# Two-layer FFN with split float32 weights: W2's high and low parts side by side in one matmul

## The reference

```python
t = cond(x)                                     # linear in x, per lane of 4 quaternion components
probs = softmax(t @ Wr.T)
h = gelu(t @ W1[7] + b1[7])                     # 256 -> 1024
out = x + (h @ W2[7] + b2[7]) * probs[:, 7:8]   # 1024 -> 256
```

## Time and profile before

| | us |
|---|---|
| median of three executions (lowest, highest) | 123.6 (123.53, 124.6) |
| span of the profiled execution, first to last instruction | 122.0 |
| TensorE matmul busy / weight loads busy | 104.4 / 92.1 |
| VectorE, ScalarE, GpSimd busy | 60.0, 49.7, 51.2 |

### The profile page before, as it was taken

The page is one execution under the profiler, slowest core; times in us unless marked ns, Lnnn a source line. Parts: engine busy times, 40 slices in busy tenths (PEclk is TensorE's granted clock), DMA queues, the critical chain, the costliest instruction groups (busy, mean ns, idle before and its releaser), DMA issues.

```text
span 122.0 us, 1804 instructions
## 1 busy us (share of the span) xinstructions
PE 104.4 (86%) x625; PEld 92.1 (76%) x625; DVE 60.0 (49%) x125; ACT 49.7 (41%) x82; POOL 51.2 (42%) x29
## 2 busy tenths in 40 slices
PE   4332999999999799999999999999999999999000
PEld 4222658899999598999998899999988999999000
DVE  1041669983489568225492972335829423335200
ACT  4000577644442447444452474444734445450000
POOL 3032004999793002975900059386000893920000
PEclk9999999999999999999999999999999999999985
DMA  0499882000000212443012034410220220000121
GB/s 21 118 253 278 243 134 42 0 0 5 0 0 21 90 63 54 100 115 79 4 44 103 24 87 122 109 26 0 70 101 16 52 79 26 0 0 0 15 91 65
DMA packets 9740, 8.09 MB, mean 66 GB/s; under 512 B 6624, under 2 KB 8424, under 8 KB 9736
## 3 DMA queue, kind: packets, MB, share of 16 engines
q1 hardware_dynamic: 9688, 7.91, 24.4%
q0 software_dynamic: 48, 0.13, 0.3%
HBM read 5.94 MB, written 2.10 MB: 66 GB/s over the span
## 4 chain that ended last, share of the span: by engine, by line
PE 77%; DMA 8%; issue 3%; DVE 2%; ACT 1%; SPq 1%; DVEq 0%; ACTq 0%
PE pre L598 35%; PE acc L604 22%; PE acc L608 11%; DMA x_in<-in_x 8%; PE lT_bank L581 3%; PE acc L567 3%; PE pre L567 1%; DVE y L442 1%; PE acc L547 1%; DVE xT_lo L424 1%; SPq L230 1%; DVE xT L431 1%; ACT h_all L340 1%; ACT xT_hi L325 1%; SPq L232 0%
## 5 line engine op out<-in xcount | busy, mean ns | idle before, releaser
L449 DVE TENSOR_TENSOR h_lo<-h_all,h_hi 128x512 fp32r<-128x512 f32 x32 | 30.0, 940 | 30.9 <-ACT h_all L340 30.9
L338 ACT ACTIVATE h_hi<-pre,b_cols 128x512 fp32r<-128x512 f32 x32 | 22.0, 687 | 40.8 <-PE pre L598 40.5
L604 PE MATMUL acc<-w_lo,h_hi 128*128 128x256 f32 x128 | 32.6, 283 | 0.0
L604 PE MATMUL acc<-w_hi,h_hi 128*128 128x256 f32 x128 | 32.5, 282 | 0.0
L604 PEld LDWEIGHTS acc<-w_hi,h_hi 128*128 128x128 f32 x128 | 24.3, 190 | 1.5 <-issue 0.3
L598 PE MATMUL pre<-xT_lo,w_hi 128*128 128x512 f32 x64 | 25.2, 394 | 0.0
L604 PEld LDWEIGHTS acc<-w_lo,h_hi 128*128 128x128 f32 x128 | 24.5, 191 | 1.0
L598 PE MATMUL pre<-xT_hi,w_hi 128*128 128x512 f32 x64 | 25.2, 394 | 0.0
L608 PE MATMUL acc<-w_hi,h_lo 128*128 128x256 f32 x128 | 22.5, 283 | 0.0
L289 POOL TENSOR_TENSOR exps<-e_const,shifted 128x32 f32<-128x32 f32 x4 | 22.1, 5514 | 0.3
L340 ACT ACTIVATE h_all<-pre,b_cols 128x512 f32<-128x512 f32 x32 | 21.8, 682 | 0.0
(11 more groups left out here) (62 smaller groups left out, 64.5 us busy)
## 6 DMA issues: line engine op xcount, KB each, us to landing
x_sq<-in_x SPq DMA_DIRECT2D x12, 128.0 KB, 5.8
x_in<-in_x SPq DMA_DIRECT2D x3, 512.0 KB
out<-y SPq DMA_DIRECT2D x3, 512.0 KB
w<-in_W SPq DMA_DIRECT2D x2, 512.0 KB, 12.3
w_cat<-in_W SPq DMA_DIRECT2D x2, 384.0 KB, 9.1
x_in<-in_x SPq DMA_DIRECT2D x2, 256.0 KB
out<-y SPq DMA_DIRECT2D x2, 256.0 KB
w_cat<-in_W SPq DMA_DIRECT2D x1, 256.0 KB, 9.1
```

The source lines that it names most:

```text
L338: nc.scalar.activation(h_hi[:, s, :], pre[f % 2][:, :], ACT.Gelu, bias=b1_cols[:, f:f + 1]).then_inc(h_hi_ready, 1)
L449: nc.vector.tensor_tensor(h_lo[:, s, :], h_all[:, s, :], h_hi[:, s, :].bitcast(F32), ALU.subtract).then_inc(h_lo_ready, 1)
L604: nc.tensor.matmul(acc[j], h_hi[:, f % SLOTS, j * P:(j + 1) * P], w[:, f, :], start=(f == 0 and w is w2_hi), stop=False)
```

## The change

w2_hi and w2_lo become one tile, w2_parts, with the high and the low part of each hidden tile next to each other ([P, FT, 2, C]). `high(f, j)` is one matmul of 512 columns over both: h_hi times the high part goes to the first half of bank acc j, h_hi times the low part to the second half. `low` adds to the first half as before. In `finish` VectorE takes two operations per token tile: part = acc_low * prob + rest, then, behind a wait for it (`part_ready`), y = acc_high * prob + part. VectorE's cast and GpSimd's difference write their results into w2_parts in rows of 256 with a step of 512.

```diff
-        w2_hi = sb("w2_hi", [P, FT, C], F32R)
-        w2_lo = sb("w2_lo", [P, FT, C], F32R)
+        w2_parts = sb("w2_parts", [P, FT, 2, C], F32R)
...
+        part = sb("part", [P, TT, C])
...
-        acc = [bank[:, 0:C] for bank in acc_banks]
+        acc = [bank[:, :] for bank in acc_banks]
+        acc_high = [bank[:, 0:C] for bank in acc_banks]
+        acc_low = [bank[:, C:2 * C] for bank in acc_banks]
...
-                nc.gpsimd.tensor_tensor(w2_lo[:, half, :], w2[:, half, :], w2_hi[:, half, :].bitcast(F32),
+                nc.gpsimd.tensor_tensor(w2_parts[:, half, 1, :], w2[:, half, :], w2_parts[:, half, 0, :].bitcast(F32),
                                         ALU.subtract).then_inc(w2_lo_ready, 1)
...
                 for j in range(TT):
                     dve.wait_ge(tile_done, TT * (b - 1) + j + 1)
                     nc.vector.scalar_tensor_tensor(
-                        out=y[:, j, :], in0=acc[j],
-                        scalar=prob[:, j:j + 1], in1=rest[:, j, :], op0=ALU.mult, op1=ALU.add).then_inc(y_ready, 1)
+                        out=part[:, j, :], in0=acc_low[j],
+                        scalar=prob[:, j:j + 1], in1=rest[:, j, :], op0=ALU.mult, op1=ALU.add).then_inc(part_ready, 1)
+                    dve.wait_ge(part_ready, TT * (b - 1) + j + 1)
+                    nc.vector.scalar_tensor_tensor(
+                        out=y[:, j, :], in0=acc_high[j],
+                        scalar=prob[:, j:j + 1], in1=part[:, j, :], op0=ALU.mult, op1=ALU.add).then_inc(y_ready, 1)
...
-                nc.vector.tensor_copy(w2_hi[:, half, :], w2[:, half, :]).then_inc(w2_hi_ready, 1)
+                nc.vector.tensor_copy(w2_parts[:, half, 0, :], w2[:, half, :]).then_inc(w2_hi_ready, 1)
...
             def high(f, j):
-                for w in (w2_hi, w2_lo):
-                    nc.tensor.matmul(acc[j], h_hi[:, f % SLOTS, j * P:(j + 1) * P], w[:, f, :],
-                                     start=(f == 0 and w is w2_hi), stop=False)
+                nc.tensor.matmul(acc[j], h_hi[:, f % SLOTS, j * P:(j + 1) * P], w2_parts[:, f, :, :],
+                                 start=(f == 0), stop=False)

             def low(f, j):
-                return nc.tensor.matmul(acc[j], h_lo[:, f % SLOTS, j * P:(j + 1) * P], w2_hi[:, f, :],
+                return nc.tensor.matmul(acc_high[j], h_lo[:, f % SLOTS, j * P:(j + 1) * P], w2_parts[:, f, 0, :],
                                         start=False, stop=(f == FT - 1))
```

More of the change, by code:

```diff
@@ L205, in adaln_ffn @@
         y_ready = sem("y_ready")
+        part_ready = sem("part_ready")
         block = ctx.enter_context(nc.Block())
```

## The result

The changed kernel took 127.2 us (median of four runs, 125.94 to 127.5) against 124.1 us for the kernel before in the same session (123.53 to 124.7): ratio 1.032, 95% interval 1.022 to 1.043. A second set of runs on one chip gave 1.025, interval 1.019 to 1.031. Both say slower. The forecast was 125.8 us, range 124.3 to 127.0: the sign and the chain of causes were right, the size too small. 127.2 lies 0.2 above the range; the median of the second set, 126.56, lies inside it. Between the medians of changed kernel and kernel before lie 3.1 us in the first set and 2.8 in the second, where the forecast had 2.2. The profiled execution, whose own time of 127.5 us is the longest of the four, has a span of 125.7 us, 3.7 more than before.

What follows compares the result with a forecast made beforehand. TensorE's chain bounded the kernel, with a VectorE and GpSimd loop only just shorter that would take over. Terms 0.63 + 0.51 + 0.27 - 0.22 + 1.03 = +2.2 us gave 125.8 us, range 124.3 to 127.0.

Steps and rivals of the forecast that it cites:

- The wait inside finish: VectorE's two steps per token tile: part to y 0.516 us, y to next part 0.395, finish 3.72 instead of 1.66.
- Rival A: The wait between finish's two steps is free: pair 0.79 us, finish 3.24, kernel +0.7, 124.3 us; chance 0.15.
- The matmul's saving: TensorE's second product: one 512-column matmul for two of 256 saves 7 ns, 0.03 us per f, bounds 0 to 12 ns.
- Second loop: VectorE and GpSimd's loop from router to router, 0.25 us to spare before, would set blocks: +0.63 and +0.51 us.
- 8.54 later: Stretch from finish's end to exps' end on VectorE and GpSimd, 8.54 us in block 2, kept unchanged in the forecast.
- extra 0.14: Block 1's old finish took 0.14 us longer (1.80); added to its new time: 24.09 against 23.46, +0.63.
- lost there: Block 0's matmul saving is lost at router(1), which already waited for xT_lo (idle 0.95 us).
- The first store's 1.03: Last block: the first store waits for two token tiles, 1.90 us instead of 0.88, +1.03.
- The extra 1.03 hides there: At the end, the second store's further 1.03 us delay hides behind the first's 2.6 us; otherwise the end is 3.25 late.
- Rival B: TensorE alone sets the blocks, router without a wait; only its waits for y and the end count: +1.3, 124.9; chance 0.17.
- C: Not slower: h_lo of f=6 gets ahead of rest and finish goes at 395 ns apiece: +0.1, 123.7 us; chance 0.05.
- D: Dearer: both successions in finish at 0.516 us, or the cast at 1.4: +3.4, 127.0, or +2.9, 126.5; chance 0.13.

Runs made afterwards that it cites:

- e2: Kernel before with finish in two dependent steps per token tile, matmuls left narrow: 126.93 us, ratio 1.029 to the kernel before.
- e4: Changed kernel with the logit transposes, sum and maximum of blocks 1 to 3 moved ahead of finish: 125.89 us, ratio 1.020 to the kernel before.
- e6: Changed kernel with one more VectorE transpose (about 0.6 us) ahead of h_lo of f=2 in blocks 1 to 3: 126.51 us, ratio 1.021 to the kernel before.
- e10: Kernel before with the logit maximum moved earlier and half of block 0's w2 low part made on VectorE: 122.99 us, ratio 0.995 to the kernel before.
- e7: Kernel before with 1.2 us of VectorE transposes inside the last finish, so only the second store is late: 124.0 us, ratio 1.001.
- e3: Changed kernel with finish in one step, the wide matmul's second half computed but not read: 122.69 us, ratio 0.992 to the kernel before.
- e5: Changed kernel with the logit maximum ahead of finish and TensorE waiting for y tile by tile: 124.68 us, ratio 1.008 to the kernel before.

## Why the prediction was right or wrong

**The sign and its causes: right.** The loop through finish, maximum, exps, prob_b, rest and the held h_lo took over from TensorE. In the changed profile every station of it is where the sum put it but one, and e2 and e4 show it from two sides: without the wide matmul the blocks stay the same, with the maximum moved they shrink.

**The wait inside finish: right.** 0.51 and 0.40 give 3.74 us for four tiles, against 3.72. Rival A, a free wait, falls: part to y is 0.11 us longer than y to the next part. The Trainium skill (VectorE: DVE Perf Modes, The DRAIN you can't avoid) found a semaphore after each operation free for eight tensor_copy. For this pair, in which each step also reads PSUM, the trace doesn't agree.

**The matmul's saving: a little low.** I took 7 ns a pair from the first product's mean; the four wide ones show 11, inside the bounds of 0 and 12. The last stretch gave back 0.12 us net, where the sum had a loss of 0.05. The Trainium skill's spacing (TensorE: Matmul & The Clock Gate, Back-to-back issue gap), which the page has for a matmul by itself, would give 2.5 ns (2.6 in the prediction is a slip); the runs are further from it than my term.

**Second loop: mis-sized by 0.32 us per block.** The step that failed is "8.54 later", the stretch from finish's end to exps' end, carried over unchanged; it measured 8.86. I moved exps and left its neighbours alone. With finish 2 us longer, h_all of f=2 is long ready, h_lo of f=2 follows that of f=1 at once, and exps runs into it. e6 separates the two and gets the 0.32 back. Block 0 of the kernel before, with its 5.78 us, could have given the price. In block 1 the old finish's extra 0.14, which I added, did not recur, so that block came out 0.17 above the sum and block 2 0.28.

**Block 0: "lost there" was too kind.** Its matmul saving is indeed lost at router(1), but it also turns round who is held, h_lo or prob_b: 0.17 us. The changed kernel's profiles have another 0.09 to 0.15 us between the first product and exps. They belong to the scatter of the start: from the first product to router(0) it is 2.82 us in the changed kernel and 2.84 in e10, which has the narrow matmuls, against 2.63 in the kernel before, and the long ones are the executions whose clock record begins late (see the last section).

**The end: two terms.** The first store's 1.03 was right (1.04). "The extra 1.03 hides there" was not: 0.45 us of it shows, and e7 makes the same 0.4 us in the kernel before.

**The start.** The strided cast and difference cost nothing: e3 has both, and its first exps starts 8.68 us behind the first product, as before; the changed kernel's two casts take 0.68 us each. The 0.43 us by which the profiled executions differ there is scatter between executions.

Together: the forecast's 2.2, plus 0.17 and 0.28 in the two blocks, 0.32 in block 0, 0.45 at the end, 0.43 of scatter, less 0.17 in the last stretch, is 3.7. Without the scatter, 0.43 and the 0.15 inside block 0, the change costs 3.1, near the 3.1 and 2.8 between the medians. The prediction's 1.6 us between median and span sets the median of three executions against the span of another; every run that lists both has its time 1.7 to 1.9 above its own span. The upper end of the range had the dearer wait and the dearer cast, neither of which came. What came was two small holds and one exposed store; the store was named, as "if it doesn't", but had no chance of its own. Rival B fell because all three routers wait and h_lo of f=6 is held; C because that h_lo starts at 85.31, inside rest (84.19 to 86.76), and the pair takes 0.91; D because the pair isn't 1.03 and the cast isn't 1.4.

## What to carry to other kernels

When a step is made longer on an engine whose operations hold another engine's, or are held by them, work out again what now runs beside each later operation: a gap that closes can cost as much as an instruction. A second chain only 1% shorter than the bounding one takes over as soon as the first gets faster or it gets longer, so a saving on the bounding engine should be counted only up to that slack. Where an operation must be added ahead of a wait, look first for idle time in the same engine's program into which something else can be moved (here the logit maximum), and weigh the last repetition by itself, since nothing covers it.

## What the runs showed of the hardware that I had not expected

- A VectorE difference of two SBUF tiles and a GpSimd operation hold each other by who starts first: h_lo 0.69 to 2.35 us behind prob_b, prob_b 1.89 to 2.40 behind h_lo, with 0.1 us deciding. The Trainium skill (SBUF — State Buffer, Who interferes with whom) says that a VectorE instruction with two SBUF inputs contends with a GpSimd instruction that reads SBUF, and that the order of issue decides who is blocked; for prob_b and rest the traces agree. GpSimd's exps (5.43 us, 32 elements) was lengthened only by an h_lo that was running at its start: the h_lo that begins 0.36 us into it takes 0.65 us, against 0.69 elsewhere. The page has the shared pair as an exclusive lock, and for exps that isn't seen.
- The scatter of the start goes with TensorE's clock. The view of windows prints a granted clock of 1.00 from the start on in every kernel, and the section on time and profile before took that for full speed. But the trace's first clock record begins only at 17.09 us in the changed kernel, at 15.59 in the kernel before and at 14.32 in e5; for the time ahead of it there is no record. At these places the weight loads of the folding matmuls go from 0.34 us to 0.19 and the distance between their starts from 0.65 to 0.33, one half. An estimate from that pace: the lower of the two levels, 1.2 GHz, up to there, and 2.4 GHz behind it. In the changed kernel's profile:

```profile
16.40 0.34 PEld L576 LDWEIGHTS acc<-w_cat,R 128*128 128x128 f32 x1 [0.32 <-issue]
17.06 0.21 PEld L576 LDWEIGHTS acc<-w_cat,R 128*128 128x128 f32 x1 [0.32 <-issue]
```

  In e5's the loads take 0.19 from 14.60 on, and the first product starts 1.65 us sooner:

```profile
14.60 0.19 PEld L580 LDWEIGHTS pre<-w_cat,R 128*128 128x128 f32 x1
14.93 1.17 PEld L580 LDWEIGHTS acc<-w_cat,R 128*128 128x128 f32 x4
```

  Over the twelve profiles the first record begins between 14.32 and 17.54 us and the first product between 16.42 and 18.33, in nearly the same order. Scatter of this kind is one reason why a single pair of executions can't tell a change of one per cent here.
- In one stream of matmuls, four of 512 columns took 227.5 ns each (L612), while L607's six take 231 at the same size and clock.
